# Layer 1 attention: probabilities weight the normalised context, and products of weights replace the value projection

## The reference, cut to what matters

```python
xn  = layernorm(ctx, ln_x_g, ln_x_b)          # 1500 context rows
ln  = layernorm(x,   ln_l_g, ln_l_b)          # 56 latent rows
q   = ln @ W_q
k,v = split(concat(xn, ln) @ W_kv)            # 1556 keys and values
q,k = rmsnorm(q, q_gamma), rmsnorm(k, k_gamma)
p   = softmax(mask(q @ k.T * 64 ** -0.5))
x   = x + (p @ v) @ W_out + b_out
```

## Time and profile before

| | us |
|---|---|
| median of 3 runs | 2246.54 (2246.37 to 2247.35) |
| the profiled execution's own time | 2248.04 |
| its span, first to last instruction | 2246.3 |
| PE busy in the span | 2102.4 (94%) |
| DVE, ACT, POOL busy | 1497.3, 1222.4, 749.4 |
| layer 1 attention in the trace | about 471 to 767 |
| mean granted clock of TensorE | 0.953 |

### The profile page before, as it was taken

One profiled execution on the slowest core, in us unless ns is written; L12 is line 12 of the kernel. 1 busy time (PEld: TensorE's weight loads), 2 busy tenths in 40 slices (PEclk: granted clock), 3 DMA queues, 4 the chain that ended last, 5 costly groups with the idle time before them and its releaser, 6 DMA issues. The chain is left out here.

```text
span 2246.3 us, 48142 instructions
## 1 busy us (share of the span) xinstructions
PE 2102.4 (94%) x19158; PEld 1551.7 (69%) x19158; DVE 1497.3 (67%) x3097; ACT 1222.4 (54%) x2377; POOL 749.4 (33%) x305
## 2 busy tenths in 40 slices
PE   6999999768999799999999999999997889999996
PEld 3677777657888545577777777777774457777774
DVE  5777777687878445466666666666635567777784
ACT  5877877535666232354444444444431367777763
POOL 6665664035656193111211112111100163443310
PEclk7999999868999799899999999999997979999998
DMA  6555454213331211112211131112000254444420
GB/s 164 144 144 153 137 146 121 69 41 118 122 120 53 58 38 48 67 59 74 102 60 59 59 109 67 59 59 92 9 1 20 79 150 131 128 149 123 139 78 9
DMA packets 94160, 199.82 MB, mean 89 GB/s; under 512 B 41729, under 2 KB 49969, under 8 KB 93682
## 3 DMA queue, kind: packets, MB, share of 16 engines
q1 hardware_dynamic: 93938, 196.74, 29.3%
HBM read 116.22 MB, written 0.65 MB: 52 GB/s over the span
## 5 line engine op out<-in xcount | busy, mean ns | idle before, releaser
L1619 PEld LDWEIGHTS L2ps<-L2probsT,L2values 125*128 125x128 f32 (+1 forms) x2688 | 317.5, 192 | 51.3 <-issue 49.2
L1600 PE MATMUL L2ps<-L2keys,L2qz 128*128 128x501 f32 x672 | 340.8, 591 | 0.9 <-DVE L2out_bias L1836 0.9
L1619 PE MATMUL L2ps<-L2probsT,L2values 125*128 125x128 f32 (+1 forms) x2688 | 318.4, 275 | 0.5 <-ACT L2probsT L1729 0.5
L1812 DVE CUSTOM_DVE_ANT_0 L2work<-L2ps,L2maskadd,L2big 128x1503 f32<-128x1503 f32 x112 | 199.5, 1781 | 74.3 <-PE L2ps L1600 74.2
L1614 PEld LDWEIGHTS L2ps<-const,L2work 128*126 128x126 f32 x1344 | 164.6, 140 | 118.6 <-issue 116.7
L1714 POOL TENSOR_TENSOR L2keys<-L2keys,L2mean_spread 127x1500 f32<-127x1500 f32 x15 | 51.5, 3432 | 578.6 <-DMA L2wqk<-L_moments 578.6
L654 ACT ACTIVATE L3probsT<-L3ps 128x448 f32<-128x448 f32 x384 | 196.3, 547 | 71.1 <-PE L3ps L511 66.3
L654 ACT ACTIVATE L0probsT<-L0ps 128x448 f32<-128x448 f32 x384 | 198.4, 552 | 47.4 <-PE L0ps L511 46.3
L1614 PE MATMUL L2ps<-const,L2work 128*126 128x128 f32 x1344 | 202.9, 274 | 3.5 <-DVE L2work L1821 3.1
L1731 ACT COPY L2qz<-L2ps 128x128 f32<-128x128 f32 x112 | 29.8, 266 | 304.9 <-PE L2ps L1619 304.9
L798 DVE TENSOR_REDUCE L0partmax<-L0ps 112x1 f32<-112x1000 f32 x128 | 153.4, 1198 | 58.3 <-PE L0ps L484 56.2
(11 more groups left out here) (470 smaller groups left out, 4283.7 us busy)
## 6 DMA issues: line engine op xcount, KB each, us to landing
L0key_stack<-L0key_parts SPq DMA_DIRECT2D x192, 187.5 KB
L3key_stack<-L3key_parts SPq DMA_DIRECT2D x192, 187.5 KB
L0ctxT<-in_ctxT SPq DMA_DIRECT2D x16, 750.0 KB, 4.4
L1raw<-in_ctx SPq DMA_DIRECT2D x16, 750.0 KB
L1rawT<-in_ctxT SPq DMA_DIRECT2D x16, 750.0 KB, 6.2
L2raw<-in_ctx SPq DMA_DIRECT2D x16, 750.0 KB
L3ctxT<-in_ctxT SPq DMA_DIRECT2D x16, 750.0 KB, 4.4
L2mean_spread<-L_moments SPq DMA_DIRECT2D x15, 750.0 KB, 6.8
```

What stands on the lines that cost most here:

```text
L1600: last = nc.tensor.matmul(PS[:, 3 * (m % 2) + c, 0:NPR], tile_rows(m), KT[:, m // RT % 2, 500 * c:500 * c + NPR], start=True, stop=True)
L1619: last = nc.tensor.matmul(PS[:, bank, 0:P], V[0:keys_in(c), i // RT % 2, c, :], PT[0:keys_in(c), i % 2, c, :], start=c == 0, stop=c == NCH ...
L1812: nc.vector.tensor_tensor_reduce(SM[:, m % 2, :].rearrange("p (c n) -> p c n", c=3), PS[:, 3 * (m % 2):3 * (m % 2) + 3, 0:NPR], MA[:, m // ...
```

## The change: what it does

The value projection of the context is gone. With centred, scaled rows the sum over keys of p * v is (sum of p * normalised row) @ (gain * W_v), plus a bias; so the kernel multiplies the probabilities with the normalised context itself, and multiplies by gain * W_v * W_out of each head at the end. The last feature's column of `V` holds ones, which carries the bias; the last row of the weights is subtracted from the others, since a centred row sums to zero. The 56 latent keys have other weights (W_v without the context's gain), so their part is kept apart: O, Z and `HT` have two halves, and Y is 4 products in place of 1.

ACT no longer empties V; in `normalise` it makes V from `RAW` in SBUF by scale (`rs`) and bias (`nm`, minus mean times `rs`, one new DVE instruction per batch), 12 instructions of 125x127. In ACT's order exp(n) now stands first and the three `normalise(n+2)` behind it, ahead of the T3 copies. T3(n, 0) is emptied by ACT where DVE did it. `RAW` has three buffers, is freed by `normalise` where the statistics freed it, and is loaded in two DMAs (112 and 13 rows).

```diff
-    units = kv(0, (0, 1, 2)) + turned_keys(0) + kv(1, (0, 1, 2))
+    units = keys(0) + turned_keys(0) + keys(1)
     for n in range(B):
         if n + 2 < B:
-            units += kv(n + 2, (0, 1, 2))
-        units += [("T3", n, j, "DAAD"[j]) for j in range(4)]
+            units += keys(n + 2)
+        units += [("T3", n, j, "AAAD"[j]) for j in range(4)]
...
     def load_raw(self, sp, b):
-        sp.dma_start(self.RAW[:, b % 2], self.src["ctx"][b]).then_inc(self.ctx_loaded[b % 2], 16)
+        for rows in (slice(0, TT), slice(TT, CH)):
+            sp.dma_start(self.RAW[rows, b % 3], self.src["ctx"][b][rows]).then_inc(self.ctx_loaded[b % 3], 16)
...
-                if b + 2 < B:
-                    sp.wait_ge(s.stats_ready, b + 1)
-                    ahead.load_raw(sp, b + 2)
+                if b + 1 < B:
+                    sp.wait_ge(s.v_ready, 3 * (b - 1))
+                    ahead.load_raw(sp, b + 1)
...
                 elif what == "O":
...
-                    last = nc.tensor.matmul(PS[0:TT, bank, 0:P], PT[0:Q, NCH, :], VL[:, b, :], start=False, stop=True)
+                    last = nc.tensor.matmul(PS[0:TT, bank, P:2 * P], PT[0:Q, NCH, :], VL[:, b, :], start=True, stop=True)
                 elif what == "Z":
                     wait_emptied(pe, plan.emptied("O", b, 0))
-                    last = nc.tensor.transpose(PS[:, bank, 0:TT], Z[:], k.ident[0:TT, 0:TT])
+                    for x in range(2):
+                        last = nc.tensor.transpose(PS[:, bank, x * TT:(x + 1) * TT], Z[:, x], k.ident[0:TT, 0:TT])
                 elif what == "Y":
-                    last = nc.tensor.matmul(PS[:, bank, 0:HALF], W[:, 3, :], HT[:, b * HALF:(b + 1) * HALF],
-                                            start=True, stop=True)
+                    for n in range(2 * H):
+                        last = nc.tensor.matmul(PS[:, bank, 0:HALF], WVO[:, n // H, n % H, :],
+                                                HT[:, n // H, n % H, b * HALF:(b + 1) * HALF], start=n == 0, stop=n == 2 * H - 1)
...
+            def normalise(b, j):
+                if j == 0:
+                    act.wait_ge(s.nm_ready, b + 1)
+                    if b >= 3:
+                        act.wait_ge(s.filled, plan.filled("O", b - 3, 0))
+                for c in range(4 * j, 4 * j + 4):
+                    last = nc.scalar.activation(V[:, b % 3, c, 0:P - 1], RAW[:, b % 3, c, 0:P - 1], ACT.Identity,
+                                                bias=nm[:, b % 2, c:c + 1], scale=rs[:, b, c:c + 1])
+                last.then_inc(s.v_ready, 1)
...
             for n in range(B):
-                if n + 2 < B:
-                    empty("V", n + 2, 0)
                 if n:
                     exp(n)
                 if n + 2 < B:
-                    empty("V", n + 2, 1)
-                    empty("V", n + 2, 2)
+                    normalise(n + 2, 0)
+                    normalise(n + 2, 1)
+                    normalise(n + 2, 2)
+                empty("T3", n, 0)
                 empty("T3", n, 1)
                 empty("T3", n, 2)
...
                 if what == "K":
                     dve.wait_ge(s.rs_ready, b + 1)
+                    if j == 0:
+                        if b >= 2:
+                            dve.wait_ge(s.v_ready, 3 * b - 3)
+                        nc.vector.scalar_tensor_tensor(nm[:, b % 2, :], k.ctx_mv[:, b, :, 0], -1.0, rs[:, b, :], ALU.mult, ALU.mult
+                                                       ).then_inc(s.nm_ready, 1)
...
-                empty("T3", n, 0)
                 empty("T3", n, 3)
```

More of the change, by code:

```diff
@@ L872, in latent_units @@
 def latent_units():
-    kv = lambda b, js: [u for j in js for u in (("K", b, j, "D"), ("V", b, j, "A"))]
+    keys = lambda b: [("K", b, j, "D") for j in range(3)]
     turned_keys = lambda b: [("T2", b, j, "ADA"[j]) for j in range(3)]
-    units = kv(0, (0, 1, 2)) + turned_keys(0) + kv(1, (0, 1, 2))
+    units = keys(0) + turned_keys(0) + keys(1)
     for n in range(B):
         if n + 2 < B:
-            units += kv(n + 2, (0, 1, 2))
-        units += [("T3", n, j, "DAAD"[j]) for j in range(4)]
+            units += keys(n + 2)
+        units += [("T3", n, j, "AAAD"[j]) for j in range(4)]
         if n + 1 < B:
@@ L990, in _ @@
         def _(sp):
-            for b in range(2, 4):
-                sp.wait_ge(s.stats_ready, b - 1)
-                ahead.load_raw(sp, b)
+            ahead.load_raw(sp, 2)
             for b in range(2, B):
-                sp.wait_ge(s.filled, plan.filled("V", b - 2, 2))
+                sp.wait_ge(s.filled, plan.filled("K", b - 2, 2))
                 ahead.load_turned(sp, b)
@@ L1008, in unit @@
                     wait_emptied(pe, plan.before(what, b, j))
-                if what in "KV":
+                if what == "K":
                     pe.wait_ge(ctxt_loaded[b % 2], 16 * (b // 2 + 1))
-                    if b == 0 and j == 1 and what == "V":
-                        pe.wait_ge(s.bias_ready, 1)
+                    if b == 0 and j == 1:
+                        pe.wait_ge(s.products_ready, 1)
                     for i in range(4):
-                        last = nc.tensor.matmul(PS[0:CH, bank, i * P:(i + 1) * P], chunk(b, 4 * j + i), WF[:, "KV".index(what), :],
+                        last = nc.tensor.matmul(PS[0:CH, bank, i * P:(i + 1) * P], chunk(b, 4 * j + i), WF[:],
                                                 start=True, stop=True)
@@ L1058, in _ @@
             pe.wait_ge(s.fold_in, 1)
[L1059 to L1063, removed]
-            ln_turn(pe, k, s, PS)
+            nc.tensor.matmul(PS[:, 7, 0:P], CEN[:], GW[:, 0], start=True, stop=True)
+            nc.tensor.matmul(PS[0:CH, 7, P:2 * P], BB[:], W[:, 1, :], start=True, stop=True)
+            nc.tensor.matmul(PS[:, 5, 2 * P:2 * P + 1], W[:, 2, :], k.v("L1_xb"), start=True, stop=True)
+            nc.tensor.transpose(PS[:, 7, 2 * P:3 * P], GW[:, 1], k.ident)
+            last = nc.tensor.transpose(PS[:, 7, 3 * P:4 * P], W[:, 2, :], k.ident)
+            last.then_inc(s.folded, 1)
+            ln_turn(pe, k, s, PS)
+            pe.wait_ge(s.turned_ready, 1)
+            for x, values in enumerate((GV, VT)):
+                for h in range(H):
+                    rows = slice(h * HD, (h + 1) * HD)
+                    last = nc.tensor.matmul(PS[:, 5 + h, x * P:(x + 1) * P], values[rows], W[rows, 3, :], start=True, stop=True)
+            last.then_inc(s.products, 1)
             pe.wait_ge(s.ln_done, 2)
@@ L1077, in _ @@
             for b in range(B):
-                last = nc.tensor.matmul(PS[0:Q, b // 4, (b % 4) * P:(b % 4 + 1) * P],
-                                        XM[:, b * Q:(b + 1) * Q], W[:, 2, :], start=True, stop=True)
+                last = nc.tensor.transpose(PS[0:Q, b // 4, (b % 4) * P:(b % 4 + 1) * P], k.xnT[:, b * Q:(b + 1) * Q], k.ident)
             last.then_inc(s.lat_v, 1)
@@ L1092, in _ @@
                 unit("K", 1, j)
-                unit("V", 1, j)
             for n in range(B):
@@ L1153, in empty @@
                 act.wait_ge(s.filled, plan.filled(what, b, j))
[L1154 to L1161, removed]
+                if what == "T2":
                     if b:
@@ L1206, in _ @@
             for j in range(3):
-                empty("V", 0, j)
+                normalise(0, j)
             squares(0)
@@ L1216, in _ @@
             mask(1)
-            empty("V", 1, 0)
+            normalise(1, 0)
             exp(0)
-            empty("V", 1, 1)
-            empty("V", 1, 2)
+            normalise(1, 1)
+            normalise(1, 2)
             squares(1)
             for n in range(B):
-                if n + 2 < B:
-                    empty("V", n + 2, 0)
                 if n:
@@ L1245, in stats @@
             def stats(b):
-                dve.wait_ge(ctx_loaded[b % 2], 16 * (b // 2 + 1))
+                dve.wait_ge(ctx_loaded[b % 3], 32 * (b // 3 + 1))
                 for c in range(NCH):
-                    last = nc.vector.bn_stats(st[:, c, :], RAW[:, b % 2, c, :])
+                    last = nc.vector.bn_stats(st[:, c, :], RAW[:, b % 3, c, :])
                 link(last)
@@ L1277, in empty @@
                 elif what == "Z":
-                    for h in range(H):
-                        p = slice(h * HD, (h + 1) * HD)
-                        ins = nc.vector.tensor_copy(HT[p, b * Q:(b + 1) * Q], PS[p, bank, h * Q:(h + 1) * Q])
+                    for x in range(2):
+                        ins = nc.vector.tensor_copy(HT[:, x, :, b * Q:(b + 1) * Q],
+                                                    PS[:, bank, x * TT:(x + 1) * TT].rearrange("p (h q) -> p h q", h=H))
                 elif what == "Y":
                     x = k.xT[:, b * HALF:(b + 1) * HALF]
-                    ins = nc.vector.scalar_tensor_tensor(x, PS[:, bank, 0:HALF], OB[:], x, ALU.add, ALU.add)
+                    ins = nc.vector.scalar_tensor_tensor(x, PS[:, bank, 0:HALF], k.v("L1_bout"), x, ALU.add, ALU.add)
```

(4 more changed lines are left out.)

43 lines of the change are left out of this document (22 added, 21 removed).

## The result

The changed kernel takes 2304.57 us (median of 4 runs, 2300.84 to 2308.95) against 2246.94 for the kernel before in the same comparison: ratio 1.0257, 95% interval 1.0235 to 1.0278. It is 57.6 us slower; forecast were 48 (2295, range 2266 to 2308). The profiled execution took 2307.03 with a span of 2305.0.

What follows compares the result with a forecast made beforehand. Two equally long chains, PE and ACT-DVE, were taken to bound the 14.23 us iteration. Terms 36 + 4 + 5.5 + 2.6 + 1 = 49 us on 2248.0 profiled gave 2297, as median 2295, range 2266 to 2308.

Steps and rivals of the forecast that it cites:

- Two chains of equal length before: Loop before the change: PE's work and the ACT-DVE chain from maximum to maximum both fill the 14.23 us iteration.
- The price of `normalise`: ACT, each SBUF-to-SBUF instruction with scale and bias columns: 0.39 us, 4.7 us for 12.
- The new chain, 16.3 us: ACT-DVE from maximum to maximum with `normalise` ahead of the T3 copies: 16.3 us, 2.1 more than 14.23.
- TensorE's stalls: PE idle per iteration: from 2.5 to 3.6 us, about 0.6 before the last T3 unit, 2.7 ahead of T2.
- The slow clock: PE's work behind the long stall runs slow in four iterations of five: 1.5 us on average, period 17.8.
- regular iteration: One of ten loop iterations, 2 to 7 and 10 to 13: each 3.6 us longer, 36 us together.
- The rule by which a gap of this length keeps the full clock: Rival: PE's 2.7 us gap in the loop keeps the full clock; period 16.3, +30, total 2277; chance 0.25.
- The rival on the faster side: TensorE alone bounds the loop: period falls to 11.6 us, total 2219; chance 0.04.
- `nm` outside the chain: DVE's small new instruction, ready at about 2.5 us after the maximum, so `normalise` doesn't wait for it.
- Y and the end: Output projection products: iteration 8 with the first Y +5.5 us, last Y +2.6, Z's wider scaling 0.1.
- The stages behind, nothing: Stages after the changed one, behind the last addition to xT: 0 us change.
- the recovering ones: Two iterations that recover from a stall (1 and 9): 15.7 us before, now 17.8, 4 us together.

Runs made afterwards that it cites:

- e6_before_t3act: Kernel before the change with only the copy T3(n, 0) emptied by ScalarE instead of VectorE: 2254.87 us, ratio 1.0033.
- e2_onecol: Changed kernel with `normalise` using the scale column alone, the bias column left out: 2283.53 us, ratio 1.0166.
- e3_warm: Changed kernel with ten matmuls that nothing reads added on TensorE between T3 and T2 of each iteration: 2296.17 us, ratio 1.0219.
- e1_late: Changed kernel with `normalise` moved in ScalarE's order behind the T3 copies, squares and T2 copies, same instructions: 2252.96 us, ratio 1.002.
- e4_t3dve: Changed kernel with T3(n, 0) emptied by VectorE again, as before the change: 2291.26 us, ratio 1.0203.
- e8_warm2: e3_warm with four more unread matmuls in the TensorE stall ahead of T3: 2293.86 us, ratio 1.0205.
- e9_warm3: e8_warm2 with two more unread matmuls behind each of the first three T3 units: 2288.01 us, ratio 1.0181.
- e5_cand: Candidate from e1_late: `V` only scaled, centring moved into the turned value weights, no `nm`, ScalarE also empties Z: 2237.05 us, ratio 0.9955.

## Why the prediction was right

- **Two chains of equal length before**: right. e6_before_t3act lengthened the ScalarE chain by one copy and the iteration by 0.43 us.
- **The price of `normalise`**: right. Forecast 0.39 each, from a row of another stage and the exp; 4.60 / 12 = 0.38 measured. (The upper bound of 0.42 had no row behind it.) The Trainium skill, "ScalarE: Activation LUTs", section "What ACT_TABLE_LOAD costs", gives the same, as an estimate from its figures: 186 ns and two columns at 93 ns, 0.83 ns per element, less 93 ns of overlap, are 385 ns for 127 elements. The 0.09 us that e2_onecol saved per instruction agrees with its second column.
- **The new chain, 16.3 us**: right. Where the clock was kept full (e3_warm) the iteration took 16.23.
- **TensorE's stalls**: nearly right; 1.01 (forecast 1.1), 0.21 ahead of the last T3 unit (0.6), 2.91 (2.7).
- **The slow clock**: mechanism right, size short. I took 1.5 us per iteration, slow stretches in four of five. They came in every regular iteration, 17.58 to 19.04 us, and cost 1.9 to 2.0: ten times 0.4 is the 4 us that the regular iterations are above the forecast. The rule by which a gap of this length keeps the full clock (the Trainium skill, "TensorE: Matmul & The Clock Gate", "Why this matters for your kernels") would have given 2277. The trace decides against it: with 2.91 us as the longest stall, the granted clock was 0.90 and 0.82 in the two iterations shown.
- **The rival on the faster side**: its turning point was 2.6 us for the 12 `normalise` *in that place*. Measured 4.6. With the place changed (e1_late) the same amount no longer held the loop. What I had not drawn from my own chain is that the loss was one of order and could be had back.
- **`nm` outside the chain**: wrong in part. It took 0.16 to 0.22 us in six of the ten regular iterations and 0.46 to 0.56 in the four others, which are just those of 19.0 us. In e1_late it took 0.74 to 1.01 in eight of ten (last section).
- **Y and the end**: right, 5.7 and 2.7 against 5.5 and 2.7.
- **The stages behind, nothing**: wrong by 3.8 us. They run the same instructions (11374 on PE in both). The first matmuls of the layer 2 attention show where part of it lies, before and after:

```profile
886.81 1.06 PE L101 MATMUL L2ps<-const,xT 128*112 128x128 f32 x8 [2.95 <-PEq L78]
```
```profile
941.94 1.93 PE L101 MATMUL L2ps<-const,xT 128*112 128x128 f32 x8 [2.95 <-PEq L78]
```

The same stall of 2.95 us ahead of the same 8 passes left the full clock in one and half of it in the other, where it stayed for some 17 us. From kernel to kernel these stages took 1476.0 (e4_t3dve) to 1486.3 us (e8_warm2) in the profiled executions. These stages are the same in every kernel here, so a few us of such differences are not the work of an edit's instructions; whether an edit sets them off by shifting when the stages start is not shown. That they also make the changed kernel's runs spread over 8 us is likely but not shown, since only one run of each kernel has a trace.
- **Luck**: little. Against the trace, the forecast was short by 0.8 us in iteration 0, 0.6 in the recovering ones, 4.3 in the regular ones, 0.2 in iteration 8 and 3.8 behind the layer. These add up and none makes good for another, so the result lies near the upper end of the range, 2308, and one of the four runs lies above it (2308.95).

## What to carry to other kernels

A busy share of 100% on one engine doesn't show that the engine alone is the bound: follow one iteration through the other engines, and if they too are gapless between two waits, there is a second bound that work must not be moved into. Work that is needed much later (here two iterations) belongs behind everything that another engine waits for now; that order was worth 51.6 us here, more than the whole projection that was removed (2.7 us in each of 14 iterations). And stalls that are opened on TensorE can cost more than their length, since the work behind them may run at half the clock: 1.9 us in each iteration here.

## What the runs showed of the hardware

- The clock fell without any single long stall: in e8_warm2 the stalls ahead of a slow stretch were three of 0.22 to 0.34 us between groups of T3 transposes, and in the iteration before three of 0.34 to 0.45. Filling these (e9_warm3) kept the full clock. Whether the idle time or the transposes between count isn't shown, since the added matmuls fill the one and thin out the other.
- One small VectorE instruction, `nm` (12 columns, both inputs in SBUF), took 0.16 to 0.22 us in most iterations of the changed kernel but 0.85 in the median in e1_late. There it ended, 712.92, just when POOL's key normalisation ended, 712.89:

```profile
712.05 0.87 DVE L1276 SCALAR_TENSOR_TENSOR L1neg_mean<-ctx_mv,L1rs 125x12 f32<-125x12 f32 x1
```
```profile
710.13 2.76 POOL L1141 TENSOR_TENSOR L1kn<-L1keys,L1rk 125x1536 f32<-125x1536 f32 x1
```

  It delays VectorE's key evictions by 0.7 us and so T3, T2 and O: that iteration took 14.0 us where one without the overlap took 13.43. The Trainium skill, "SBUF — State Buffer", section "SBUF: two separate sides", says that a VectorE instruction with two SBUF inputs and a GpSimd instruction that reads SBUF exclude each other for the whole instruction; the two ends agree with it. In the changed kernel `nm` was held up by 0.3 to 0.4 us in four regular iterations, 584.00 to 584.55 for one beside POOL's 581.76 to 584.52. These four took 19.0 us, the six others 17.58 to 17.87, and the slow stretch was longer in them (granted clock 0.82 against 0.90 in those of 2 to 7). How a delay of 0.4 makes the slow stretch longer is not shown. e5_cand has no `nm`.
